# A four-layer convolution kernel: the 25 depthwise taps of its first attention as ScalarE products summed on GpSimd

## The reference

```python
lepe = lax.conv_general_dilated(v_ch, lepe_w, window_strides=(1, 1), padding='SAME', feature_group_count=C, ...) + lepe_b[:, None, None]
...
res = softmax(q k^T * SCALE) v   # per head
out = einsum(proj_w, (res + lepe) * o) + proj_b
```

## Time and profile before

| | us |
|---|---|
| three timed runs, median | 10546.03 |
| their range | 10542.94 to 10552.59 |
| the profiled execution, its own time | 10569.52 |
| its span between first and last instruction | 10567.7 |
| TensorE clock granted, mean over the span | 0.778 of full |

### The profile page before, as it was taken

One profiled execution on the slowest core, in us unless ns is written; L12 is line 12 of the kernel. 1 busy time (PEld: TensorE's weight loads), 2 busy tenths in 40 slices (PEclk: granted clock), 3 DMA queues, 4 the chain that ended last, 5 costly groups with the idle time before them and its releaser, 6 DMA issues.

```text
span 10567.7 us, 101292 instructions
## 1 busy us (share of the span) xinstructions
PE 7395.8 (70%) x33720; PEld 3735.7 (35%) x33720; DVE 8085.9 (77%) x5526; ACT 4057.7 (38%) x4186; POOL 4790.4 (45%) x1990
## 2 busy tenths in 40 slices
PE   5666777677767777677775876767776777767556
PEld 1124333433234333443333432344323433244333
DVE  4447888768886788867888689876888778887992
ACT  2233444334433344334443344433454334433431
POOL 1225564345553455434554356443554345543660
PEclk8676777787878888688776887878787878868657
DMA  1036456644476445754457444674456644575782
GB/s 36 9 118 215 156 175 222 201 164 168 161 248 196 151 160 190 238 191 142 164 188 252 157 157 168 211 225 162 163 169 235 197 164 161 187 234 197 254 268 50
DMA packets 717963, 1875.98 MB, mean 178 GB/s; under 512 B 258897, under 2 KB 274641, under 8 KB 717265
## 3 DMA queue, kind: packets, MB, share of 16 engines
q1 hardware_dynamic: 717392, 1869.00, 53.5%
HBM read 1772.03 MB, written 71.04 MB: 174 GB/s over the span
## 4 chain that ended last, share of the span: by engine, by line
PE 41%; DVE 31%; issue 14%; ACT 7%; DMA 4%; DVEq 2%; SPq 1%; ACTq 1%; POOL 0%; POOLq 0%
DVE R L1651 14%; PE ps L749 8%; DVE ps L1641 7%; PE ps L878 7%; PE ps L975 5%; ACT R L1169 4%; DVE nmx L1571 3%; PE ps L1060 3%; PE ps L887 3%; PE ps L858 3%; PE ps L948 2%; PE ps L1043 2%; PE ps L958 1%; PE ps L843 1%; PE ps L1032 1%
## 5 line engine op out<-in xcount | busy, mean ns | idle before, releaser
L1340 POOL TENSOR_TENSOR R<-R 128x1024 f32<-128x1024 f32 x1536 | 3676.4, 2394 | 4304.6 <-DVE ps L1641 4194.3
L1651 DVE TENSOR_TENSOR_SCAN R<-R,ps 128x1024 f32<-128x1024 f32 x1536 | 3507.8, 2284 | 178.9 <-ACT R L1228 65.8
L1228 ACT ACTIVATE R<-R,negA 128x1024 f32<-128x1024 f32 x1536 | 1749.2, 1143 | 2306.1 <-DVE R L1651 2268.4
L975 PE MATMUL ps<-ident,R 128*128 128x128 f32 x12288 | 2153.8, 336 | 584.0 <-POOL R L1340 542.2
L975 PEld LDWEIGHTS ps<-ident,R 128*128 128x128 f32 x12288 | 1806.8, 175 | 1576.1 <-issue 784.0
L1641 DVE TENSOR_TENSOR ps<-R 128x1024 f32<-128x1024 f32 x1536 | 2025.4, 1319 | 163.0 <-DMA R<-bc_scratch 56.7
L1169 ACT ACTIVATE R<-ps 128x1024 f32<-128x1024 f32 x768 | 784.7, 1022 | 1184.0 <-PE ps L878 1184.0
L858 PE MATMUL ps<-R 32*128 32x512 f32 x3072 | 687.3, 979 | 754.6 <-DVE nmx L1571 662.3
L1571 DVE TENSOR_REDUCE nmx<-ps 128x4 f32<-128x2048 f32 x384 | 877.0, 2284 | 298.8 <-PE ps L858 295.2
L878 PE MATMUL ps<-R 64*128 64x512 f32 x3072 | 917.8, 676 | 204.9 <-ACT R L1169 107.2
L749 PE MATMUL ps<-R 128*128 128x512 f32 (+1 forms) x1824 | 875.3, 638 | 202.2 <-DVE R L1507 142.6
(11 more groups left out here) (156 smaller groups left out, 5622.2 us busy)
## 6 DMA issues: line engine op xcount, KB each, us to landing
R<-bc_scratch SPq DMA_DIRECT2D x3072, 512.0 KB, 4.6
R<-in_x SPq DMA_DIRECT2D x72, 512.0 KB, 7.1
out<-R SPq DMA_DIRECT2D x72, 512.0 KB, 5.2
R<-shift_scratch SPq DMA_DIRECT2D x48, 640.0 KB, 7.6
R<-R SPq DMA_DIRECT2D x192, 128.0 KB
R<-out SPq DMA_DIRECT2D x48, 512.0 KB, 8.4
R<-in_w_qkvo SPq DMA_DIRECT2D x32, 576.0 KB, 6.8
rows_scratch<-R SPq DMA_DIRECT2D x24, 512.0 KB, 7.4
```

What stands on the lines that cost most here:

```text
L975: mm = pe.matmul(ps[:, 4 + b // 4, (b % 4) * P:(b % 4 + 1) * P], state[i % HELD][:, b * P:(b + 1) * P], ident[:, :], start=fresh and i % G ...
L1228: act.activation(decay[i % len(decay)], dt[:, c, :], ACT.Exp, scale=negA[:, col:col + 1]).then_inc(a_sb.h, 1)
L1340: pool.tensor_tensor(state[i % HELD], state[i % HELD], rows_c[slot], ALU.mult).then_inc(hc_sb.h, 1)
L1651: v.tensor_tensor_scan(h, a, b, 0.0, ALU.mult, ALU.add).then_inc(h_sb.h, 1)
```

## The change

All 25 taps go the way that the first 14 went: `dp` on ScalarE and `dw` on GpSimd, at 0.96 step apart from the start of S, so that the last sum is placed 24.3 steps after the group's start. The multiply-adds on VectorE (`dv`) are gone, and the semaphore that told their end. `O` no longer adds its quotient to `heads`; it leaves it in `rinv` and does not wait for the sums. A new event `oa` at the end of a group waits for the last sum and adds the group's two quotients, which lie side by side, to `heads` in one instruction of 1024. `pv` of the next group waits for the last `dw` in place of the last `dv`.

```diff
--- before.py
+++ after.py
@@ -55,7 +55,7 @@
 PER = STEPS1 // K
 AHEAD = 1.25
 S_STEPS, N_STEPS, T_STEPS = 14, 1.6, 16.2
-TAPS, SUMMED = 25, 14
+TAPS = 25
 
 
 def place(i):
@@ -196,14 +196,13 @@
         for n in range(SB):
             t = at + n * S_STEPS / SB
             ev += [(t, ("S", SB * g + n)), (t + 0.24, ("R", SB * g + n))]
-        for j in range(SUMMED):
-            t = at + 0.3 + (S_STEPS - 0.6) * j / SUMMED
+        for j in range(TAPS):
+            t = at + 0.3 + 24 * j / TAPS
             ev += [(t, ("dp", g, j))] + ([(t + 1.0, ("dw", g, j))] if j else [])
         ev += [(at + (3.0 if g == 0 else 0.3), ("q2", g))]
         at += S_STEPS
         ev += [(at - 0.1, ("N", g)), (at + 0.5, ("M", g)), (at + 0.55, ("mr", g))]
         at += N_STEPS
-        ev += [(at + 0.7 + T_STEPS * j / (TAPS - SUMMED), ("dv", g, SUMMED + j)) for j in range(TAPS - SUMMED)]
         apart = T_STEPS / TB
         for j in range(TB):
             t = at + apart * j
@@ -213,6 +212,7 @@
             if j % (TB // 2) == TB // 2 - 1:
                 ev += [(t + 2 * apart + 0.2, ("O", 2 * g + j // (TB // 2)))]
         at += T_STEPS + 1.2
+        ev += [(at - 0.1, ("oa", g))]
     ev += [(at - 0.3 + 0.5 * c, ("xb", c)) for c in range(NC)] + [(at + 1.1, ("wg",))]
     ev += [(at + 2.9 + 0.5 * c, ("xr", c)) for c in range(NC)]
     ev += [(at + 3.1, ("xn",))]
@@ -471,11 +471,10 @@
         t_ps = sem("scoresT_ready", GROUPS0 * TB, 401)
         t_exp = sem("probsT_ready", GROUPS0 * TB, 401)
         pv_ps = sem("products_done", GROUPS0 * TB // 2)
-        dp_sb = sem("tap_product_ready", SUMMED * GROUPS0)
-        dw_sb = sem("tap_summed", (SUMMED - 1) * GROUPS0)
-        dv_sb = sem("depthwise_term_ready", GROUPS0)
+        dp_sb = sem("tap_product_ready", TAPS * GROUPS0)
+        dw_sb = sem("tap_summed", (TAPS - 1) * GROUPS0)
         o_sb = sem("heads_divided", 2 * GROUPS0)
-        o_sum = sem("heads_ready", 2 * GROUPS0)
+        o_sum = sem("heads_ready", GROUPS0)
         vz_sb = sem("padding_zeroed", 1)
         lv_ps = sem("v_transposed", NC)
         lv_sb = sem("v_padded", NC)
@@ -1149,7 +1148,7 @@
                         act.activation(k4[:, i - 3, :], banks(2 * (i % 2)), ACT.Identity, bias=vec("bk", i - 3))\
                             .then_inc(qk_sb.h, 1)
                 if kind == "dp":
-                    m, n = a, (SUMMED - 1) * a + j
+                    m, n = a, (TAPS - 1) * a + j
                     win = vpad.rearrange("p (h w) -> p h w", w=36)[:, j // 5:j // 5 + HH, j % 5:j % 5 + WW]
                     tap = lepe_w[:, m * TAPS + j:m * TAPS + j + 1]
                     if j == 0:
@@ -1172,7 +1171,7 @@
                     act.wait_ge(lv_ps.h, lv_ps.at(img, m + 1))
                     act.wait_ge(vz_sb.h, vz_sb.at(img, 1))
                     if m:
-                        act.wait_ge(dv_sb.h, dv_sb.at(img, m))
+                        act.wait_ge(dw_sb.h, dw_sb.at(img, (TAPS - 1) * m))
                     inner = vpad.rearrange("p (h w) -> p h w", w=36)[:, 2:34, 2:34]
                     act.activation(inner, banks(2).rearrange("p (h w) -> p h w", w=WW), ACT.Identity, bias=vec("bv", m))\
                         .then_inc(lv_sb.h, 1)
@@ -1341,9 +1340,9 @@
 
             def early(img, kind, m=0, j=0):
                 if kind == "dw":
-                    n = (SUMMED - 1) * m + j
+                    n = (TAPS - 1) * m + j
                     pool.drain()
-                    pool.wait_ge(dp_sb.h, dp_sb.at(img, SUMMED * m + j + 1))
+                    pool.wait_ge(dp_sb.h, dp_sb.at(img, TAPS * m + j + 1))
                     pool.tensor_tensor(heads[:, m, :], heads[:, m, :], tapped[n % 2], ALU.add).then_inc(dw_sb.h, 1)
 
             def late(img, kind, u=0):
@@ -1571,25 +1570,15 @@
                     v.tensor_reduce(nmx4[:, :, qc, hf], ps[:, 0:4, :], AX.X, ALU.max, negate=True)\
                         .then_inc(s_max.h, 1)
                 if kind == "O":
-                    g, qh = a // 2, a % 2
-                    part = heads[:, g, qh * HALF:(qh + 1) * HALF]
                     v.wait_ge(pv_ps.h, pv_ps.at(img, LB * (a + 1)))
-                    v.wait_ge(dw_sb.h, dw_sb.at(img, (SUMMED - 1) * (g + 1)))
                     v.reciprocal(rinv[a], ps[:, 3, :])
                     v.drain()
                     v.tensor_tensor(rinv[a], ps[:, 2, :], rinv[a], ALU.mult).then_inc(o_sb.h, 1)
+                if kind == "oa":
+                    pair = side(2 * HALF * a, 2 * HALF)
                     v.drain()
-                    v.tensor_tensor(part, part, rinv[a], ALU.add).then_inc(o_sum.h, 1)
-                if kind == "dv":
-                    m = a
-                    out = heads[:, m, :].rearrange("p (h w) -> p h w", w=WW)
-                    win = vpad.rearrange("p (h w) -> p h w", w=36)[:, j // 5:j // 5 + HH, j % 5:j % 5 + WW]
-                    v.drain()
-                    if j == SUMMED:
-                        v.wait_ge(dw_sb.h, dw_sb.at(img, (SUMMED - 1) * (m + 1)))
-                    ins = v.scalar_tensor_tensor(out, win, lepe_w[:, m * TAPS + j:m * TAPS + j + 1], out, ALU.mult, ALU.add)
-                    if j == TAPS - 1:
-                        ins.then_inc(dv_sb.h, 1)
+                    v.wait_ge(dw_sb.h, dw_sb.at(img, (TAPS - 1) * (a + 1)))
+                    v.tensor_tensor(heads[:, a, :], heads[:, a, :], pair, ALU.add).then_inc(o_sum.h, 1)
                 if kind == "N":
                     v.wait_ge(s_max.h, s_max.at(img, SB * (a + 1)))
                     v.tensor_reduce(negm[:, :].rearrange("p (r j) -> p r j", r=GH)[:, :, 0:LB], nmx4, AX.X, ALU.min)\
```

## The result

The changed kernel took **10601.4 us** (median; 10596.6 to 10610.1), the kernel before 10547.3 us on the same chip: ratio 1.0054, 95% interval 1.0041 to 1.0066, so 54 us slower. That lies in the forecast's range (10515 to 10630), but on the side of "slower" (0.38), not in its likeliest case.

A forecast was written before the change was run, and what follows sets the result against it. In stage T the chain of waits was TensorE and ScalarE, with VectorE only at O. Terms -4, +4 and +9 us, carried to the median of 10546.0, gave 10555 us; range 10515 to 10630.

The forecast's parts named there:

- slower: ScalarE's queue, first half of T: products before an E wait for GpSimd; +79 us, half if every second misses; slower 0.38.
- likeliest case: Whole kernel: no change that the measurement can tell (about 0.2%, 21 us); chance 0.50.
- Removing VectorE's multiply-adds is worth nothing in T.: Stage T, 21 groups beside a scan: the chain does not pass through the multiply-adds, so removing them is costed at nothing.
- The -4 us of group 1: Second half of group 1, images 2 to 6: VectorE was 0.8 us late at O; five such groups, -4 us.
- The order of events stays as it was: 0.: Stage S: with taps 0.96 step apart in place of 0.957, the events keep their order; 0.
- The quotients, +4 us.: VectorE before the gate stage: one add of 1024 replaces the adds of 512; 0.54 us, 7 times, +4 us.
- The products fit behind an odd E; GpSimd's adds fit.: First half of T: nine ScalarE products fit the gap behind odd E, at nothing; GpSimd's work makes 50 of 57 us.
- The +9 us for one missed fit in each group: Untested fits between four engines: one missed 0.42 us per group, 21 groups, +9 us.
- VectorE's relief is given back by the exclusive lock.: First half of T: GpSimd's adds hold VectorE's b, up to 21 us per group, about what the multiply-adds gave back; hidden.
- b is first in N, 0.: Stage N: VectorE's b starts before GpSimd's new add, by 0.15 us; 0, or 2.35 us per group if not.
- No DMA and no queue order of SP changes.: SP's queue: loads of C wait for GpSimd's multiplications, three steps ahead, and stay hidden; no term in the sum.
- they are costed at nothing; their cover is TensorE's own 5.33 us period: Stage T in 21 groups: removed multiply-adds cost nothing, covered by TensorE's 5.33 us period for two T.

The follow-up runs named there:

- e1: The changed kernel with the products and adds of taps 14 to 24 left out: 10584.5 us, ratio 1.0025 to the kernel before.
- e4: The kernel before with the quotients added once at the group's end, multiply-adds still on VectorE: 10550.3 us, ratio 0.9997.
- e5: The changed kernel with its 25 taps laid over 31 steps of the group instead of 24: 10590.8 us, ratio 1.0039 to the kernel before.
- e9: e4 with 9 taps in S, 11 in N and first half of T, five multiply-adds left on VectorE: 10567.2 us, ratio 1.0014 to the kernel before.
- e8: The kernel before with one unused matmul of 512 columns ahead of each group's first T: 10510.3 us, ratio 0.9961.

## Why the prediction was right or wrong

- **Removing VectorE's multiply-adds is worth nothing in T.** Right in what it says of VectorE: the same half at full clock is 43.98 us with them and without. Wrong in the sum: e1 against e4 shows 34 us for their removal together with the swap on ScalarE. The -4 us of group 1 came: its second halves last 44.0 us in all seven images, where six of them had 44.7. But e4 has them at 44.0 as well, so it was the add of O that was in the way, not the multiply-adds.
- **"The order of events stays as it was: 0."** Not so: the last product of S and the decay beside it changed places (section on e4). What that costs was not measured by itself.
- **The quotients, +4 us.** Right within the measurement (e4: 0.9997).
- **The products fit behind an odd E; GpSimd's adds fit.** Right: no idle time before a product in T, 51.0 us of GpSimd where 50 was worked out, TensorE's idle time up by 2.8 us over 21 groups. The +9 us for one missed fit in each group was about 6 too much.
- **VectorE's relief is given back by the exclusive lock.** Right in kind: b rose by 0.2 us on average (1.32 to 1.52), 314 us in all, of the 513 removed; hidden in T, where the wait at O shows the slack.
- **b is first in N, 0.** Right for group 2, on which it was argued (first in all seven), wrong for group 1, which I had not looked at: held in 6 of 7, +7.5 us over the 21 groups from N to M, and by the multiplication, not by the new add as I had feared. e1, without late adds, has it in 5 of 7.
- **"No DMA and no queue order of SP changes."** The order is the same, yet in group 2 the first T comes 0.8 us later behind M (5.3 for 4.55). Why was not tried.
- **The step that failed, in a forecast whose range held, is the sum: it has no term for TensorE's clock.** It held "they are costed at nothing; their cover is TensorE's own 5.33 us period", and took that period for a constant. It is the busy time of matmuls, which is 1.13 us for a T at one level and 2.08 at the other. The change, put at nothing here, brought 33 us of busy time in T (e4's trace to the changed kernel's). The earlier trace rows had the column: 0.96 in the first half, 1.00 in the second, that is 4 to 5 us of low clock in one half of one group. T stages at +23 us (against e4's trace +36) are all of this kind but 3.
- **The slower rival** had the side and nearly the size (+79, half of it 40), by a mechanism that took place in no run: not one product in T waits for GpSimd, in e5 and e9 either. e5 shows what the price would buy: with products in front of E in a full ScalarE queue, 39 us of idle time. The chance of 0.38 for slower was thus right for a wrong reason.
- **The range** held because its upper bound was made for the slower rival; a change of the low time in T from 99 to 231 us, which these runs span, is worth 66 us and was in no bound.

The Trainium skill, TensorE: Matmul & The Clock Gate, HAM oscillation — how this bites in real kernels, says that waits between bursts of matmuls can put the array back to half rate each time, and charges half of the time spent there as the loss. The traces agree with the charge: 75 us more of low time between e4 and the changed kernel, 32.9 us more busy time; 76 us less in e8, 31.4 less. That it is waits that put the array back agrees too for the stretches begun inside T: each began at a wait of 1.4 to 3.0 us or just behind it (where ScalarE holds E back, and at O). The stretch at the start of T is mostly another: it began in S.

**What stays open.** Why the low time in T is 221 us in e1 and 155 in e4, and whether it is the missing multiply-adds or the swap on ScalarE that does it; a kernel with e1's edit and the taps 0.957 step apart would tell. TensorE's waits in T are the same in sum. That their place decides, and what ran before them, is a guess: the longer wait ahead of T (36.5 to 46.4 us) is shown, but most of the added low time lies further in. That the late products and adds add the other half of the loss is what the medians say (30 us for e1, 54 for all); the traces of the two differ by 3 us of span, so how they do it isn't settled either.

## What to carry to other kernels

Read the granted clock beside TensorE's busy time for each stage, and compare busy time at equal instruction counts before blaming a wait: a stage that TensorE bounds has two lengths. Freeing an engine that does not bound a stage is not sure to be free of cost: here the time rose with it, and neither busy shares nor waits foretold it. Where events get a new spacing, however little, compare the order of each engine's queue before and after. Where TensorE must wait for a short transfer ahead of a dense stage, one cheap unused matmul in the wait is worth trying: 0.4% here on two versions, 0.2% and nothing that can be told on two others.

## What the runs showed of the hardware

- Four matmuls of 64 x 512 in f32 (one T): 1.13 us at the upper level, 2.08 at the lower. 276 matmuls of one half: 47.72 us at 1.00, 51.50 at 0.93.
- One unused matmul per group (two instructions in the trace, about 1 us together) in a wait that had been 1.4 us or more left 99 us of low time in 21 stages in place of 175, and 106 in place of 155 on the other base.
- A two-operand SBUF instruction of VectorE that begins just after one of GpSimd ends about 1.1 us after that one: b 3.11 us for 1.23, the multiply-add 3.44 for 1.28. With 264 more adds of 2.68 us on GpSimd the 1536 drives took 314 us longer.
